# Issuing the load of the next input chunk at the top of a pipelined iteration instead of at its end

## The chip, the cores and the metric

The kernel runs on the eight NeuronCores of one Trainium2 chip. Each core gets two of the sixteen sequences of the input (2 x 2048 rows of 1024 numbers) and works alone; there is no traffic between cores. The metric is the device time in microseconds of the slowest core. A core has a tensor engine (PE), a vector engine (DVE), a scalar engine (ACT), GpSimd (POOL) and a sync engine (SP), which here does nothing but issue DMAs, in the order of its program.

## The reference

```python
xn = _layernorm(x, axis=-1)
s = _L0_attn_ref(xn, Wq, Wk, Wv, Wo)      # 16 heads of 64, causal window of 128, banded softmax
g = _silu(_L0_ffn_ref(xn, rhs))           # rows and columns scaled by absmax/127, rounded, product, rescaled
x = x + s * g
```

In `_L0_attn_ref`, q, k and v are `xn @ W.T`; a chunk of 128 queries looks at its own 128 keys and at the 128 before, under a band mask; the attention output goes through `Wo`. The input is 16 x 2048 x 1024 in float32.

## The kernel before

**Tiling.** A chunk is 128 rows of x, so a core has 32 chunks. All five weight matrices stay in SBUF as bf16. A chunk has five products of 128 x 1024 by 1024 x 1024, each written as 16 matmuls of 128x512: q, k and v (line 461, into `p_proj`, from `wbf`), the quantised product, called ffn (line 461, from `qrhs`), and the output projection, called op (line 565, into `p_av`). Scores (lines 478 and 483, into `p_sc`) and the product of probabilities and values (lines 497 to 506, 64 small matmuls, called AVS) lie between them.

**Order.** There is no scheduler: every engine has its own program, written out by hand, one loop over i from -2 to 33 in each. In iteration i an engine finishes chunk i and prepares chunks i+1, i+2 and i+3. Engines meet at counting semaphores: `W(engine, name, tag)` waits until the counter has reached the value that stands for that step.

- PE: scores of heads 0 to 7 of chunk i, q of i+1, scores of heads 8 to 15, k of i+1, AVS of i, v of i+1, ffn of i+1, op of i. AVS waits for the masks of DVE, v waits for ACT's copy of k out of `p_proj` (line 406), ffn for ACT's copy of v (line 428).
- DVE: the two mask multiplications of chunk i (line 324), reciprocal and scaling of the attention output (lines 329, 333), LN2 of chunk i+2 (lines 256 to 280: inverse deviation by Newton steps on single columns, then the normalised rows `xn`), the ffn product's scaling (342), the combination of chunk i (351, 355: output = x + s g), the gate (362), and LN1 of chunk i+3 (lines 233 to 248: sum, centring, absolute maximum, quantisation factor). LN1 begins with a wait for the load of x of that chunk. LN2 waits for ACT's sum of squares (421).
- ACT: exponentials of the scores (381, 394), copy of q (387), after q's transpose the two copies into zero-padded halves (400, 402), copy of k (406), quantisation of chunk i+2 (415, 418), squares (421), copy of v (428), tanh (433).
- SP: transposes of q (line 174, called trq), of the attention output (180, trao), of k (186, trk), of the quantised rows (194, trql), of the normalised rows (198, trxn), then the store of chunk i (205) and the load of x of chunk i+3 (214). Each waits for the engine that makes its source. All of them lie in one queue.

x has a ring of four slots `XS` in SBUF, chunk c in slot c % 4. The loads of chunks 0, 1 and 2 are issued ahead of the loop.

The helper through which every wait goes is line 126, the one for issues is line 130 to 136.

Of the kernel before, what the change touches and what calls it, by code (L numbers as in the profile page):

```python
# [20 lines left out]
XS = [0, 1024, 2048, 3072]  # L21
# [52 lines left out]
def build(nchunk=NCHUNK):  # L74
    nc = bass.Bass("TRN2", target_bir_lowering=False)
    x_h = nc.dram_tensor("x", [2, 2048, D], F32, kind="ExternalInput").ap()
# [13 lines left out]
    with ExitStack() as es:  # L90
# [3 lines left out]
        scr = sb("scr", [128, SCR_COLS], F32)  # L94
# [26 lines left out]
        def ap3(tensor, cols, off):  # L121
            return bass.AP(tensor, off, [[cols, 128], [128, 8], [1, 128]])

        def W(eng, sname, tag):
            if CUR[0].emit:
                eng.wait_ge(SEMS[sname], CUR[0].tag[(sname, tag)])
# [5 lines left out]
        def I(instr, sname=None, tag=None, n=1):  # L132
            if CUR[0].emit:
                bi = instr()
                if sname is not None:
                    bi.then_inc(SEMS[sname], n)
            if sname is not None:
                CUR[0].inc(sname, n, tag)


        def emit_sync(sync):
            I(lambda: sync.dma_start(mstd[:], mstd_h[:]), "ldw", None, 16)
            I(lambda: sync.dma_start(mc0[:], mc0_h[:]), "ldw", None, 16)
            I(lambda: sync.dma_start(onesc[:], ones_h[:]), "ldw", None, 16)
            I(lambda: sync.dma_start(ident[:], ident_h[:]), "ldw", None, 16)
            I(lambda: sync.dma_start(sel[:], sel_h[:]), "ldw", None, 16)
            I(lambda: sync.dma_start(scr[:, XS[0]:XS[0] + 1024], x_h[0, 0:128, :]),
              "lx0", ("x", 0), 16)
            for i in range(8):
                if i >= 2:  # L150
                    W(sync, "v", ("cast", i - 2))
                wst = WST[i % 2]
                src = rhst_h[i * 128:(i + 1) * 128, :]
                I(lambda src=src, wst=wst: sync.dma_start(scr[:, wst:wst + 1024], src),
                  "ldw", ("ldw", i), 16)
            W(sync, "v", ("cast", 7))
            for ntile in range(8):
                out_ap = bass.AP(qrhs, ntile * 128, [[8192, 128], [1024, 8], [1, 128]])
                in_ap = ap3(bfp2, BFP2_COLS, QRHS_T + ntile * 1024)
                I(lambda o=out_ap, ii=in_ap: sync.dma_start_transpose(o, ii),  # L160
                  "trs", ("trs", ntile), 16)
            for c in (1, 2):
                if c < nchunk:
                    b1, cc1 = divmod(c, 16)
                    I(lambda b1=b1, cc1=cc1, c=c: sync.dma_start(
                        scr[:, XS[c % 4]:XS[c % 4] + 1024],
                        x_h[b1, cc1 * 128:(cc1 + 1) * 128, :]),
                      f"lx{c % 4}", ("x", c), 16)

            for i in range(-2, nchunk + 2):  # L170
                if 0 <= i + 1 < nchunk:
                    c = i + 1
                    W(sync, "a", ("qte", c))
                    I(lambda c=c: sync.dma_start_transpose(
                        ap3(bfp, BFP_COLS, QTF), ap3(bfp, BFP_COLS, QROW)),
                      f"trq{c % 2}", ("trq", c), 16)
                if 0 <= i < nchunk:
                    c = i
                    W(sync, "v", ("ao", c))
                    I(lambda c=c: sync.dma_start_transpose(  # L180
                        ap3(bfp2, BFP2_COLS, AOT[c % 2]), ap3(bfp2, BFP2_COLS, AO[c % 2])),
                      f"trao{c % 2}", ("trao", c), 16)
                if 0 <= i + 1 < nchunk:
                    c = i + 1
                    W(sync, "a", ("kte", c))
                    I(lambda c=c: sync.dma_start_transpose(
                        ap3(bfp, BFP_COLS, KT[c % 2]), ap3(bfp, BFP_COLS, KROW)),
                      f"trk{c % 2}", ("trk", c), 16)
                if 0 <= i + 2 < nchunk:
                    c = i + 2  # L190
                    if i >= 0:
                        W(sync, "t", ("ffn", i))
                    W(sync, "a", ("qbf", c))
                    I(lambda c=c: sync.dma_start_transpose(
                        ap3(bfp, BFP_COLS, QLT[c % 2]), ap3(bfp, BFP_COLS, QB[c % 2])),
                      f"trql{c % 2}", ("trql", c), 16)
                    W(sync, "v", ("xn", c))
                    I(lambda c=c: sync.dma_start_transpose(
                        ap3(bfp, BFP_COLS, XNT[c % 2]), ap3(bfp, BFP_COLS, XN[c % 2])),
                      f"trxn{c % 2}", ("trxn", c), 16)  # L200
                if 0 <= i < nchunk:
                    c = i
                    b, cc = divmod(c, 16)
                    W(sync, "v", ("comb", c))
                    I(lambda b=b, cc=cc, c=c: sync.dma_start(
                        y_h[b, cc * 128:(cc + 1) * 128, :],
                        scr[:, OUTS[c % 2]:OUTS[c % 2] + 1024]),
                      "st", ("store", c), 16)
                if 3 <= i + 3 < nchunk:
                    c = i + 3  # L210
                    if i >= 1:
                        W(sync, "v", ("comb", i - 1))
                    b1, cc1 = divmod(c, 16)
                    I(lambda b1=b1, cc1=cc1, c=c: sync.dma_start(
                        scr[:, XS[c % 4]:XS[c % 4] + 1024],
                        x_h[b1, cc1 * 128:(cc1 + 1) * 128, :]),
                      f"lx{c % 4}", ("x", c), 16)
            if CUR[0].emit:
                sync.wait_ge(SEMS["st"], 16 * nchunk)

# [362 lines left out]
        class FakeEng:  # L583
            def __getattr__(self, name):
                raise RuntimeError("pass-1 must not touch the engine")
        fe = FakeEng()
        emit_sync(fe)
        emit_vector(fe)
        emit_scalar(fe)
# [8 lines left out]
        @block.sync  # L598
        def _(sync):
            emit_sync(sync)  # L600
# [58 lines left out]
```

## Time and profile before

| | us |
|---|---|
| median of 3 runs | 1088.12 (1085.11 to 1091.45) |
| the profiled execution | 1089.02 |
| its span (slowest core, core 6) | 1087.5 |
| spans of the eight cores | 1070.6 to 1087.5 |
| busy on core 6: PE, DVE, ACT | 757.0, 522.6, 424.5 |
| mean granted TensorE clock, cores | 0.906 to 0.912 |

The span runs from the first to the last instruction. Busy shares of engines are averages over the whole span; the clock is a share of 2.4 GHz, so 0.50 is the 1.2 GHz level. A number in square brackets at the end of a timeline row is how long the engine was idle ahead of the instruction, with what ended it. One period of the loop is read from one line of ACT (428, once a chunk) to the same line of the next chunk.

### The profile page before, as it was taken

What the parts mean: (1) busy time and instruction counts of PE and PEld (TensorE: products, weight loads), DVE (VectorE), ACT (ScalarE), POOL (GpSimd) and SP (SyncE); (2) the same over time, 40 slices, a digit from 0 to 9 for tenths busy, and PEclk for the clock granted to TensorE, in tenths of its full rate; (3) what the DMA queues carried; (4) which work ended last, traced back from release to release, by engine and by line L of the source; (5) the groups of instructions that cost most, each with busy time, mean ns of one, the idle gap of its engine ahead of it and who ended that gap; (6) DMA issues with size and microseconds to landing.
All of it is one profiled execution on the core that took longest, in us unless ns stands there. A gap on an engine that the chain in (4) does not pass through costs nothing.

```text
span 1087.5 us, 15213 instructions; the slowest of 8 cores (1070.6 to 1087.5 us)
## 1 busy us (share of the span) xinstructions
PE 757.0 (70%) x5649; PEld 398.9 (37%) x5649; DVE 522.6 (48%) x984; ACT 424.5 (39%) x385; POOL 17.4 (2%) x36
## 2 busy tenths in 40 slices
PE   0001687787787777777788777777877788777794
PEld 0001243343344433434344443444444344433442
DVE  4234254544445544554444554555545544544533
ACT  0001354444334444444443434444444334444441
POOL 6000000000000000000000000000000000000000
PEclk9999998889988988988998988988899988988896
DMA  8964334234433333432434333433233334343321
GB/s 161 186 125 106 79 58 88 71 69 85 87 88 72 75 69 87 88 73 65 88 87 88 82 62 72 88 88 82 67 76 88 87 88 79 74 63 87 88 49 49
DMA packets 193048, 91.40 MB, mean 84 GB/s; under 512 B 179272, under 2 KB 179656, under 8 KB 192976
## 3 DMA queue, kind: packets, MB, share of 16 engines
q1 hardware_dynamic: 188368, 82.04, 34.4%
q0 software_dynamic: 4608, 8.39, 5.2%
q8 instruction: 46, 0.75, 0.3%
q14 instruction: 26, 0.21, 0.1%
HBM read 37.98 MB, written 16.78 MB: 50 GB/s over the span
## 4 chain that ended last, share of the span: by engine, by line
PE 47%; DMA 19%; DVE 19%; ACT 7%; issue 5%; SPq 3%; DVEq 1%; ACTq 0%
PE p_proj L461 28%; DMA scr<-x 11%; PE p_av L565 10%; DMA scr<-rhst 5%; DMA bfp<-bfp 4%; PE p_av L497 4%; PE p_av L503 3%; DVE bfp L324 3%; ACT bfp L428 3%; DVE scr L355 3%; DVE scr L351 3%; DVE sm L243 2%; DVE sm L233 2%; DVE scr L239 2%; SPq L160 1%
## 5 line engine op out<-in xcount | busy, mean ns | idle before, releaser
L461 PE MATMUL p_proj<-wbf,bfp 128*128 128x512 bf16 x1536 | 390.9, 413 | 32.8 <-DMA bfp<-bfp 15.0
L461 PEld LDWEIGHTS p_proj<-wbf,bfp 128*128 128x128 bf16 x1536 | 155.6, 105 | 230.7 <-issue 97.6
L497 PE MATMUL p_av<-bfp 128*128 128x64 bf16 x512 | 81.5, 213 | 146.3 <-DVE bfp L324 143.9
L461 PE MATMUL p_proj<-qrhs,bfp 128*128 128x512 bf16 x512 | 115.6, 379 | 43.8 <-ACT bfp L428 43.8
L497 PEld LDWEIGHTS p_av<-bfp 128*128 128x128 bf16 x512 | 64.4, 126 | 160.3 <-issue 160.0
L565 PE MATMUL p_av<-wbf,bfp 128*128 128x512 bf16 x512 | 118.5, 386 | 5.0 <-DMA bfp<-bfp 5.0
L233 DVE TENSOR_REDUCE sm<-scr 128x1 f32<-128x1024 f32 x32 | 39.0, 1220 | 147.0 <-DMA scr<-x 147.0
L433 ACT ACTIVATE scr<-scr 128x1024 f32<-128x1024 f32 x32 | 33.8, 1056 | 174.1 <-DVE scr L342 174.1
L342 DVE SCALAR_TENSOR_TENSOR scr<-p_proj,sm,scr 128x1024 f32<-128x1024 f32 x32 | 41.1, 1284 | 124.8 <-PE p_proj L461 124.8
L428 ACT CAST bfp<-p_proj 128x1024 bf16<-128x1024 f32 x32 | 32.4, 1012 | 161.6 <-PE p_proj L461 161.6
L461 PEld LDWEIGHTS p_proj<-qrhs,bfp 128*128 128x128 bf16 x512 | 47.8, 97 | 111.6 <-issue 58.6
L381 ACT ACTIVATE bfp<-p_sc 128x2048 bf16<-128x2048 f32 x32 | 60.0, 1877 | 58.5 <-PE p_sc L483 56.3
L503 PE MATMUL p_av<-bfp 128*128 128x64 bf16 x512 | 81.8, 213 | 0.0
L506 PE MATMUL p_sc<-ones_s,bfp 128*128 128x1 bf16 x512 | 81.0, 188 | 0.0
L500 PE MATMUL p_sc<-ones_s,bfp 128*128 128x1 bf16 x512 | 80.8, 188 | 0.0
L415 ACT ACTIVATE q32t<-scr,sm 128x1024 int32<-128x1024 f32 x32 | 36.7, 1148 | 101.9 <-DVE bfp L302 91.9
L351 DVE TENSOR_TENSOR scr<-p_av,scr 128x1024 f32<-128x1024 f32 x32 | 39.2, 1225 | 77.0 <-PE p_av L565 77.0
L565 PEld LDWEIGHTS p_av<-wbf,bfp 128*128 128x128 bf16 x512 | 50.7, 99 | 67.4 <-issue 8.8
L324 DVE TENSOR_TENSOR bfp<-bfp,mstd_s 128x2048 bf16<-128x2048 bf16 x60 | 71.0, 1222 | 4.5 <-ACT bfp L394 4.2
L478 PE MATMUL p_sc<-bfp 128*128 128x128 bf16 x512 | 64.5, 220 | 2.2 <-ACT bfp L381 2.2
L439 PE MATMUL p_av<-ident_s,sm 128*8 128x128 f32 x1 | 0.4, 373 | 94.3 <-DVE bfp L302 94.3
L503 PEld LDWEIGHTS p_av<-bfp 128*128 128x128 bf16 x512 | 65.0, 127 | 0.0
(58 smaller groups left out, 903.6 us busy)
## 6 DMA issues: line engine op xcount, KB each, us to landing
scr<-x SPq DMA_DIRECT2D x32, 512.0 KB, 4.8
y<-scr SPq DMA_DIRECT2D x32, 512.0 KB, 3.0
scr<-rhst SPq DMA_DIRECT2D x8, 512.0 KB
bfp<-bfp SPq DMA_TRANSPOSE x160, 3.3
wbf<-wqt POOLq DMA_DIRECT2D x8, 256.0 KB, 14.9
wbf<-wkt POOLq DMA_DIRECT2D x8, 256.0 KB, 26.1
wbf<-wvt POOLq DMA_DIRECT2D x8, 256.0 KB, 36.5
wbf<-wot POOLq DMA_DIRECT2D x8, 256.0 KB, 47.3
```

Of the source, the lines that this page charges most:

```text
L233: SW(lambda c=c: vector.reduce_sum(sm[:, SUMC:SUMC + 1], scr[:, XS[c % 4]:XS[c % 4] + 1024], AX.X))
L324: I(lambda e=ebv, r=erv, m=mkv: vector.tensor_tensor(e, r, m, ALU.mult), "v", ("e0m" if g == 0 else "e1m", c))
L351: SW(lambda c=c: vector.tensor_tensor(scr[:, T1_:T1_ + 1024], p_av[:, 0:1024], scr[:, GS[c % 2]:GS[c % 2] + 1024], ALU.mult))
L381: I(lambda: scalar.activation(bfp2[:, ERAW:ERAW + 2048], p_sc[:, 0:2048], AF.Exp, scale=0.125), "a", ("e0", c))
L428: I(lambda c=c: scalar.copy(bfp[:, VS[c % 2]:VS[c % 2] + 1024], p_proj[:, 0:1024]), "a", ("vev", c))
L461: mms.append(lambda kc=kc, half=half: tensor.matmul(p_proj[:, half * 512:(half + 1) * 512], lhs_t[:, lhs_base + kc * 128:lhs_base + kc * 1 ...
L478: mms.append(lambda hh=hh, qcol=qcol, tcol=tcol: tensor.matmul(p_sc[:, hh * 256:hh * 256 + 128], bfp[:, ktp + tcol:ktp + tcol + 128], bfp[ ...
L497: mms.append(lambda h=h, e0=e0: tensor.matmul(p_av[:, h * 64:h * 64 + 64], bfp2[:, e0:e0 + 128], bfp[:, vp_ + h * 64:vp_ + h * 64 + 64], s ...
L500: mms.append(lambda h=h, e0=e0: tensor.matmul(p_sc[:, h:h + 1], bfp2[:, e0:e0 + 128], onesc[:], start=True, stop=False))
L503: mms.append(lambda h=h, e0=e0: tensor.matmul(p_av[:, h * 64:h * 64 + 64], bfp2[:, e0 + 128:e0 + 256], bfp[:, vc_ + h * 64:vc_ + h * 64 + ...
L506: mms.append(lambda h=h, e0=e0: tensor.matmul(p_sc[:, h:h + 1], bfp2[:, e0 + 128:e0 + 256], onesc[:], start=False, stop=True))
L565: mms.append(lambda kc=kc, half=half, c=c: tensor.matmul(p_av[:, half * 512:(half + 1) * 512], bfp2[:, AOT[c % 2] + kc * 128:AOT[c % 2] + ...
```

## The change

The block of SP's program that loads x of chunk i+3 moves from the end of iteration i to its start. Its own wait stays the same: slot (i+3) % 4 was last read by the combination of chunk i-1.

```diff
             for i in range(-2, nchunk + 2):
+                if 3 <= i + 3 < nchunk:
+                    c = i + 3
+                    if i >= 1:
+                        W(sync, "v", ("comb", i - 1))
+                    b1, cc1 = divmod(c, 16)
+                    I(lambda b1=b1, cc1=cc1, c=c: sync.dma_start(
+                        scr[:, XS[c % 4]:XS[c % 4] + 1024],
+                        x_h[b1, cc1 * 128:(cc1 + 1) * 128, :]),
+                      f"lx{c % 4}", ("x", c), 16)
                 if 0 <= i + 1 < nchunk:
                     c = i + 1
                     W(sync, "a", ("qte", c))
...
                       "st", ("store", c), 16)
-                if 3 <= i + 3 < nchunk:
-                    c = i + 3
-                    if i >= 1:
-                        W(sync, "v", ("comb", i - 1))
-                    b1, cc1 = divmod(c, 16)
-                    I(lambda b1=b1, cc1=cc1, c=c: sync.dma_start(
-                        scr[:, XS[c % 4]:XS[c % 4] + 1024],
-                        x_h[b1, cc1 * 128:(cc1 + 1) * 128, :]),
-                      f"lx{c % 4}", ("x", c), 16)
```

Only SP's order differs; the programs of PE, DVE, ACT and POOL are the same. In the changed file the load is line 176, and the other lines of SP stand 9 further on: trq 183, trao 189, trk 195, trql 203, trxn 207, the store 214.

SP's queue before, from the transposes of iteration -1 to the first trao and trk of iteration 1:

```order
L174 DMA_TRANSPOSE bfp<-bfp 128x8x128 [waits s_a]
L180 DMA_TRANSPOSE bfp2<-bfp2 128x8x128 [waits s_v]
L186 DMA_TRANSPOSE bfp<-bfp 128x8x128 [waits s_a]
L194 DMA_TRANSPOSE bfp<-bfp 128x8x128 [waits s_t,s_a]
L198 DMA_TRANSPOSE bfp<-bfp 128x8x128 [waits s_v]
L205 DMA y<-scr 128x1024 [waits s_v]
L214 DMA scr<-x 128x1024
L174 DMA_TRANSPOSE bfp<-bfp 128x8x128 [waits s_a]
L180 DMA_TRANSPOSE bfp2<-bfp2 128x8x128 [waits s_v]
L186 DMA_TRANSPOSE bfp<-bfp 128x8x128 [waits s_a]
```

The load in these rows is the one of chunk 3; it stands behind the store of chunk 0. The same stretch of SP's queue after the change (trq, trao, trk, trql and trxn are L183, L189, L195, L203 and L207):

```order
L176 DMA scr<-x 128x1024
L183 DMA_TRANSPOSE bfp<-bfp 128x8x128 [waits s_a]
L189 DMA_TRANSPOSE bfp2<-bfp2 128x8x128 [waits s_v]
L195 DMA_TRANSPOSE bfp<-bfp 128x8x128 [waits s_a]
L203 DMA_TRANSPOSE bfp<-bfp 128x8x128 [waits s_t,s_a]
L207 DMA_TRANSPOSE bfp<-bfp 128x8x128 [waits s_v]
L214 DMA y<-scr 128x1024 [waits s_v]
L176 DMA scr<-x 128x1024 [waits s_v]
L183 DMA_TRANSPOSE bfp<-bfp 128x8x128 [waits s_a]
L189 DMA_TRANSPOSE bfp2<-bfp2 128x8x128 [waits s_v]
L195 DMA_TRANSPOSE bfp<-bfp 128x8x128 [waits s_a]
```

The load of chunk 3 now stands ahead of the first iteration's transposes, and behind the store of chunk 0 stands the load of chunk 4. From there on the kind of every row is the same as before; each load is of one chunk later than the load that stood there. 29 loads (chunks 3 to 31) are moved.

## Rows read from the trace of the kernel before

**Rows 1.** Waits, whole span: engine line <- releaser: us in total, times, longest.
```profile
DVE sm L233 <- DMA scr<-x: 147.0, 31, 8.6
PE p_av L497 <- DVE bfp L324: 143.9, 29, 6.6
ACT bfp L400 <- DMA bfp<-bfp: 68.2, 32, 3.7
```

**Rows 2.** Chain that ended last, one period: start us, us, what.
```profile
634.33 5.02 PE p_proj L461 x16
...
640.70 3.61 PE p_proj L461 x16
644.32 3.47 PE p_av L565 x16
...
651.01 4.81 DMA scr<-x
...
655.92 1.23 DVE sm L233
...
660.12 1.24 DVE bfp L324
661.36 0.24 issue
...
664.30 5.40 PE p_proj L461 x16
```

**Rows 3.** Timeline of ACT, same period: start us, us, instruction, idle before.
```profile
652.21 1.01 ACT L387 CAST bfp<-p_proj 128x1024 bf16<-128x1024 f32 x1 [1.52 <-PE p_proj L461]
...
657.01 1.04 ACT L400 COPY bfp<-bfp 64x1024 bf16<-64x1024 bf16 x1 [1.97 <-DMA bfp<-bfp]
...
659.13 1.01 ACT L406 CAST bfp<-p_proj 128x1024 bf16<-128x1024 f32 x1
```

**Rows 4.** Timeline of ACT, first and last periods: copies of k and v.
```profile
149.47 1.01 ACT L406 CAST bfp<-p_proj 128x1024 bf16<-128x1024 f32 x1
...
154.34 1.01 ACT L428 CAST bfp<-p_proj 128x1024 bf16<-128x1024 f32 x1 [0.29 <-PE p_proj L461]
...
1028.30 1.01 ACT L428 CAST bfp<-p_proj 128x1024 bf16<-128x1024 f32 x1 [5.78 <-PE p_proj L461]
...
1052.27 1.01 ACT L428 CAST bfp<-p_proj 128x1024 bf16<-128x1024 f32 x1 [3.85 <-PE p_proj L461]
```

**Rows 5.** Timeline of PE, iteration 0: v and the start of ffn.
```profile
150.63 3.61 PE L461 MATMUL p_proj<-wbf,bfp 128*128 128x512 bf16 x16 [1.00 <-ACT bfp L406]
155.60 0.59 PE L461 MATMUL p_proj<-qrhs,bfp 128*128 128x512 bf16 x2 [1.36 <-ACT bfp L428]
```

**Rows 6.** Timeline of DVE, iteration -1 to 0: LN1, masks, LN2.
```profile
141.69 1.21 DVE L233 TENSOR_REDUCE sm<-scr 128x1 f32<-128x1024 f32 x1
...
145.89 2.36 DVE L324 TENSOR_TENSOR bfp<-bfp,mc_s 128x2048 bf16<-128x2048 bf16 x2
...
154.15 0.15 DVE L256 TENSOR_SCALAR sm<-sm 128x1 f32<-128x1 f32 x1 [2.82 <-ACT scr L421]
```

**Rows 7.** Timeline of DVE, the period of rows 2: the gate.
```profile
650.42 1.22 DVE L362 SCALAR_TENSOR_TENSOR scr<-scr 128x1024 f32<-128x1024 f32 x1
```

**Rows 8.** Timeline of SP's queue, iteration 0: trxn.
```profile
158.67 1.23 SPq L198 DMA_TRANSPOSE bfp<-bfp  x1
```

**Rows 9.** Stretches: length, PE busy (instructions), granted clock, DMA share, GB/s.
```profile
148.00:149.00 1.00, 1.00 (x42) 1.00 0.00 0
611.00:623.00 12.00, 12.00 (x79) 1.00 0.37 90
657.00:661.00 4.00, 0.00 (x0) 1.00 0.00 0
662.00:663.00 1.00, 1.00 (x30) 0.50 0.09 16
```

**Rows 10.** Line 461 over the whole span: ns min/median/max, first and last start.
```profile
L461 PE MATMUL p_proj<-wbf,bfp x1536: 376/379/634, 113.9 to 1051.8; 128*128 128x512 bf16 x192
```

## The prediction

> **What bounds the kernel now.** I read the totals of waits first. The vector engine (DVE) waits 147.0 us for loads of x at line 233, and the tensor engine (PE) waits 143.9 us at AVS for the masks of DVE [rows 1]. The two totals are nearly alike, about 4.7 and 5.0 us a time, which suggests one cause seen from two engines. The chain of waits shows it for one period [rows 2]: op ends at 647.79 (644.32 + 3.47), the load of x is issued at 651.01 and takes 4.81, LN1 begins at 655.92, the first mask at 660.12, and AVS at 661.60 (after 0.24 of issue). In program order DVE has LN1 of chunk i+3 ahead of the masks of chunk i+1, so a load issued too late for LN1 holds masks that need nothing of it. DVE had been free since 651.64 [rows 7].
>
> The length of a period comes from ACT's copy of v: from 154.34 to 1028.30 there are 29 periods [rows 4], so 873.96 / 29 = 30.14 us each. The last period, 1028.30 to 1052.27, has no load and no LN1 and takes 23.97 [rows 4].
>
> A second loss hangs on the first. PE is idle from 657 to 661 at a granted clock of 1.00 (2.4 GHz), and in 662 to 663, inside AVS, the clock is 0.50 (1.2 GHz) [rows 9]. It comes back only within the v product: from v to ffn this period needs 640.70 - 634.33 = 6.37 us [rows 2], while in iteration 0, where the clock stayed at 1.00 in AVS [rows 9], it was 155.60 - 150.63 = 4.97 [rows 5]. That is 1.40 us.
>
> **The change, part by part.** It removes and adds no instruction. It moves 29 DMA issues, and of the other engines none. Queued behind the moved load is the whole of SP's program. Its wait, for the combination of chunk i-1, is one that the store just ahead of it has already waited for, so in the loop it adds no waiting. Between the store and the next trq there stands one load before and one after; only its chunk is one later. So the loop's DMA traffic keeps its places, and I price the move itself at 0 per period. Bounds: if it added one more issue on trq's way it would cost the 0.4 us or less that lies between neighbouring issues; it could give that back too. The one load really added at a new place is that of chunk 3, ahead of iteration 0's trq; it could hold that trq by a load's time at most, 4.81 us once [rows 2], and not by less than 0. I take 0, because PE and SP are still in iteration -1 when it goes, and keep 5 us for the range.
>
> What goes is LN1's wait, since the load is issued a period earlier. Now the new period, counted from the end of op (0). DVE frees itself at 651.64 - 647.79 = 3.85 [rows 2, 7]. LN1 takes 660.12 - 655.92 = 4.20 and the first mask 1.24 [rows 2], to 9.29; with 0.24 of issue AVS could start at 9.53. What is late next? The k product: the copy of q ends at 653.22, which is 5.43 after op [rows 3]; with a start 0.15 later (the same step as from line 406 to v, 150.48 to 150.63 [rows 4, 5]) and 3.61 of work, it ends at 9.19. So AVS starts at 9.53, and even at its length of now, 2.70 (661.60 to 664.30), it ends at 12.23.
>
> Then v waits for ACT's copy of k, and this path sets the end:
> - op's end to the end of the copy of q: 5.43.
> - From there to the start of line 400, which is trq's trip: 653.22 to 657.01 is 3.79 with 1.97 of idle [rows 3]. Over all chunks the idle time is 68.2 / 32 = 2.13 [rows 1], so 3.79 + 0.16 = 3.95.
> - Lines 400, 402 and 406, 657.01 to 660.14: 3.13 [rows 3]. To v: 0.15.
> - So v starts at 12.66, 0.43 after AVS. v to ffn at full clock: 4.97 [rows 5]. ffn and op, 640.70 to 647.79: 7.09 [rows 2].
>
> Sum: 5.43 + 3.95 + 3.13 + 0.15 + 4.97 + 7.09 = 24.72 us, against 30.14. The saving is 5.42, of which 1.40 is the clock and 4.02 the masks. Of the 147.0 us of wait about 4.0 of each 4.7 turn into time; the rest is the new wait for the copy of k.
>
> Three things were hidden by LN1's wait and stand nearly bare now. They happened in iteration 0, where x was there already (LN1 starts at 141.69 without a wait [rows 6]), so their room can be read there, counted from the end of the copy of k, 150.48:
> - The copy of v waits 0.29 for PE [rows 4], so ACT is just in time.
> - LN2 now waits for the squares of ACT (2.82, beginning at 154.15 [rows 6]). The normalised rows leave for trxn at 158.67 [rows 8], which is 8.19. ffn ends at 0.15 + 4.97 + 3.61 = 8.73, so DVE is ready for it.
> - trxn is issued at 8.19; with the trip of trq, 3.79, it has landed by 11.98. The next q starts at 0.15 + 4.97 + 7.09 + (652.21 - 647.79 - 3.61 = 0.81) = 13.02. It has 1.0 us left, where today it has over 4.
>
> The clock: in the new period PE is idle for 0.34 ahead of AVS, at most 1.3 ahead of v, and 1.36 between v and ffn, nowhere the 4 us after which it fell. A 12 us stretch in which PE was busy throughout has a clock of 1.00 [rows 9]. The Trainium skill, "TensorE: Matmul & The Clock Gate" (Part 1: The HAM clock gate), has a rule that speaks against this: with three or more cores of a die in dense matmuls, a peak-current limiter takes the die to 13/16 of the clock. The trace doesn't show it, though all eight cores run dense stretches; by the rule, as an estimate from that page, four products on the path would each be 16/13 as long, about 3.2 us more a period and some 1025 us in all.
>
> **The sum.** 29 periods x 5.42 = 157.1 us. The periods at both ends and the tail behind the last one stay. The profiled execution took 1089.0, so 1089.0 - 157.1 = 931.9: I forecast 932 us. The median of the runs shown is 1088.1, less than 0.1% away, and is not corrected for.
>
> A check: the last period, 23.97, is nearly the new one with trq alone on the queue. All periods like that would give 1089.0 - 29 x 6.17 = 910, which is the lower bound.
>
> **Rivals.**
> 1. The clock still falls once a period, because AVS is light work for PE or the remaining gaps count. Then v to ffn stays at 6.37, the period is 26.12 and the time 1089.0 - 29 x 4.02 = 972. For it: the clock is at 0.50 in just this place now. Against it: it was 1.00 in AVS of iteration 0.
> 2. The transfers collide more. trq shares SP's queue with the load just ahead of it, and the loop asks for the same bytes in less time. If every trq idled like the longest, 3.7 instead of 2.13 [rows 1], that is 1.57 a period: 932 + 46 = 978.
> 3. Power, in part: PE on all cores is busier, and the clock drops within the products. A matmul of line 461 lasts 634 ns at worst against 379 [rows 10]; 16 of them are 4.1 us a product, and four products on the path 16.3 us a period. With a sixth of that work at 1.2 GHz the period grows by 2.7, to 1011 us. The skill's limiter would be this rival.
> 4. The other side, slower: the same mechanism, in more than a third of the products' work (5.42 / 16.3); at all of it the time is 932 + 29 x 16.3 = 1405. For it speaks only that the chip has never shown a loop with so little idle time here; against it the 12 us at 1.00 [rows 9].
> 5. The change does nothing, because the masks are really released by ACT: line 406 ends at 660.14 [rows 3], the first mask starts at 660.12 [rows 2]. Then the time is 1089. Against it: a mask waits only for an exponential, and in iteration 0 the masks (145.89 [rows 6]) came well ahead of line 406 (149.47 [rows 4]).
>
> **Chances.** Forecast 0.72 (its own range 915 to 952: the bound below with the 5 us, and 0.7 us a period above), clock 0.10, collisions 0.06, power in part 0.06, slower 0.02, nothing 0.03, something else that is still faster 0.01. A measurement of this kernel tells a change of about 0.5% from none. Faster by more: 0.72 + 0.10 + 0.06 + 0.06 + 0.01 = 0.95; within: 0.03; slower: 0.02. The range of 915 to 978 holds the first three cases for the most part, and leaves out power, nothing and slower.
>
> **What would show it.** Right: the wait of line 233 for x is near zero in the loop; PE's long wait at AVS for masks falls below 1 us a time; PE now waits for ACT's copy of k (line 406) ahead of v, some 0.4 to 1.3 us a time; DVE waits for the squares at line 256; the clock is 1.00 throughout the loop; the copy of v comes every 24.7 us. Wrong: a clock under 1.00 in the loop (rivals 1, 3, 4), a wait at line 400 well over 2.1 us (rival 2), or a q product that waits for trxn, which the margin of 1.0 us should prevent.

## The result: 946.1 us where 932 was forecast, and the profile after

| | before | after |
|---|---|---|
| median of 10 runs each, us | 1087.4 (1082.7 to 1091.5) | 946.1 (942.3 to 948.8) |
| ratio, 95% interval | | 0.870 (0.868 to 0.872) |
| the profiled execution, us | 1089.0 | 946.2 |
| its span, slowest core | 1087.5 (core 6) | 944.7 (core 5) |
| spans of the cores | 1070.6 to 1087.5 | 933.1 to 944.7 |
| mean granted clock | 0.906 to 0.912 | 0.969 to 0.973 |

The kernel is 13.0% faster. The time lies in the stated range (915 to 978), 14 us above the point. In the sessions of the experiments some executions took longer with one die at a lower granted clock (one of e3 1025.0 us against 925.1), and every median below leaves them out. The waits of the changed kernel on core 5, whole span, are the first thing to read (who waited, for whom, us in total, times, longest):

```profile
DVE sm L256 <- ACT scr L421: 101.4, 31, 16.8
...
ACT bfp L400 <- DMA bfp<-bfp: 63.9, 32, 3.4
...
PE p_proj L461 <- ACT bfp L406: 33.8, 32, 2.7
...
DVE sm L233 <- DMA scr<-x: 13.0, 2, 7.6
...
PE p_av L497 <- DVE bfp L324: 8.7, 29, 0.6
```

Against [rows 1], the wait of line 233 for x went from 147.0 to 13.0 us and happens only twice, ahead of the loop; the wait of AVS for the masks went from 143.9 to 8.7, at most 0.6 a time. In their place stand the two waits that the prediction named: PE for the copy of k (line 406) and DVE for the squares of ACT (line 256).

The chain that ended last shows one period, from the copy of v to the copy of v (start, us, what):

```profile
233.00 1.02 ACT bfp L428
...
234.26 3.61 PE p_proj L461 x16
237.88 3.45 PE p_av L565 x16
...
242.22 3.47 PE p_proj L461 x16
...
245.77 1.02 ACT bfp L387
...
246.85 3.56 DMA bfp<-bfp
...
251.54 1.04 ACT bfp L402
...
252.61 1.02 ACT bfp L406
...
253.77 3.63 PE p_proj L461 x16
...
257.47 1.02 ACT bfp L428
```

The load of x, LN1 and the masks, which stood in the chain of [rows 2], aren't in it. The path is the one of the sum: ffn, op, q, copy of q, trq, lines 400 to 406, v. This period is 24.47 us. Not all are. Two neighbouring v products of the timeline of PE, and the granted clock in stretches that hold them (columns as in rows 9):

```profile
227.60 5.30 PE L461 MATMUL p_proj<-wbf,bfp 128*128 128x512 bf16 x16 [1.05 <-ACT bfp L406]
...
253.77 3.61 PE L461 MATMUL p_proj<-wbf,bfp 128*128 128x512 bf16 x16 [0.94 <-ACT bfp L406]
```

```profile
155.00:886.00 731.00, 643.06 (x5106) 0.97 0.43 94
...
227.00:228.00 1.00, 0.40 (x2) 1.00 0.00 0
228.00:231.00 3.00, 3.00 (x9) 0.51 0.51 98
...
250.00:258.00 8.00, 6.17 (x83) 1.00 0.29 56
```

The clock still fell to 1.2 GHz, now in 11 of the 29 periods on cores 4 and 5 and in 9 on the other six, and not during AVS but at the start of v. Ahead of this v PE had been idle for 1.05 us only; over all 11 falls of core 5 that gap was 1.04 to 2.40 us, and in its 18 other periods 0.29 to 0.99. On the other cores falls came with gaps from 0.39 us on. On core 5 such a v takes 5.1 to 5.3 us instead of 3.6. Both ends of the loop on core 5 are in the timeline of ACT, from which the mean period is (886.22 - 155.40) / 29 = 25.20 us:

```profile
155.40 1.01 ACT L428 CAST bfp<-p_proj 128x1024 bf16<-128x1024 f32 x1 [0.29 <-PE p_proj L461]
...
886.22 1.01 ACT L428 CAST bfp<-p_proj 128x1024 bf16<-128x1024 f32 x1 [0.29 <-PE p_proj L461]
```

### The profile page after: what moved, and what is told of

It is laid out like the page before. It is cut to its first block, busy times and chain, and to the rows that moved or that the text cites. A ratio compares the mean times of both kernels' runs of the same rounds, so it can differ in the third digit from the quotient of the medians.

```text
span 944.7 us, 15213 instructions; the slowest of 8 cores (933.1 to 944.7 us)
## 1 busy us (share of the span) xinstructions
PE 719.6 (76%) x5649; PEld 373.9 (40%) x5649; DVE 522.7 (55%) x984; ACT 424.5 (45%) x385; POOL 17.4 (2%) x36
## 4 chain that ended last, share of the span: by engine, by line
PE 52%; DMA 18%; ACT 15%; issue 6%; DVE 5%; SPq 2%; ACTq 0%; DVEq 0%
PE p_proj L461 37%; DMA bfp<-bfp 13%; PE p_av L565 12%; DMA scr<-rhst 6%; ACT bfp L402 4%; ACT bfp L406 3%; ACT bfp L428 3%; ACT bfp L387 3%; PE p_sc L478 1%; PE p_sc L483 1%; SPq L160 1%; DVE sm L292 1%; ACT bfp L400 1%; DVE scr L297 1%; DVE q32t L300 1%
## 5 line engine op out<-in xcount | busy, mean ns | idle before, releaser
L461 PE MATMUL p_proj<-wbf,bfp 128*128 128x512 bf16 x1536 | 369.4, 396 | 62.7 <-ACT bfp L406 33.8
L461 PEld LDWEIGHTS p_proj<-wbf,bfp 128*128 128x128 bf16 x1536 | 149.6, 101 | 246.4 <-issue 100.9
L381 ACT ACTIVATE bfp<-p_sc 128x2048 bf16<-128x2048 f32 x32 | 60.0, 1876 | 58.5 <-PE p_sc L483 56.3
L497 PE MATMUL p_av<-bfp 128*128 128x64 bf16 x512 | 61.4, 190 | 11.7 <-DVE bfp L324 8.7
L478 PE MATMUL p_sc<-bfp 128*128 128x128 bf16 x512 | 64.0, 219 | 2.2 <-ACT bfp L381 2.2
L483 PE MATMUL p_sc<-bfp 128*128 128x128 bf16 x512 | 64.0, 219 | 0.0
L400 ACT COPY bfp<-bfp 64x1024 bf16<-64x1024 bf16 x32 | 33.5, 1046 | 63.9 <-DMA bfp<-bfp 63.9
L503 PE MATMUL p_av<-bfp 128*128 128x64 bf16 x512 | 61.4, 190 | 0.0
L256 DVE TENSOR_SCALAR sm<-sm 128x1 f32<-128x1 f32 x32 | 4.9, 154 | 101.4 <-ACT scr L421 101.4
L394 ACT ACTIVATE bfp<-p_sc 128x2048 bf16<-128x2048 f32 x32 | 60.1, 1877 | 1.4 <-PE p_sc L483 1.4
L497 PEld LDWEIGHTS p_av<-bfp 128*128 128x128 bf16 x512 | 49.5, 97 | 27.4 <-issue 24.7
```

The costliest lines, as they stand in the source:

```text
L381: I(lambda: scalar.activation(bfp2[:, ERAW:ERAW + 2048], p_sc[:, 0:2048], AF.Exp, scale=0.125), "a", ("e0", c))
L394: I(lambda: scalar.activation(bfp2[:, ERAW + 2048:ERAW + 4096], p_sc[:, 0:2048], AF.Exp, scale=0.125), "a", ("e1", c))
L400: I(lambda c=c: scalar.copy(bfp[0:64, QTM[c % 2]:QTM[c % 2] + 1024], bfp[0:64, QTF:QTF + 1024]))
L461: mms.append(lambda kc=kc, half=half: tensor.matmul(p_proj[:, half * 512:(half + 1) * 512], lhs_t[:, lhs_base + kc * 128:lhs_base + kc * 1 ...
L478: mms.append(lambda hh=hh, qcol=qcol, tcol=tcol: tensor.matmul(p_sc[:, hh * 256:hh * 256 + 128], bfp[:, ktp + tcol:ktp + tcol + 128], bfp[ ...
L483: mms.append(lambda hh=hh, qcol=qcol, tcol=tcol: tensor.matmul(p_sc[:, hh * 256 + 128:hh * 256 + 256], bfp[:, ktc + tcol:ktc + tcol + 128] ...
```

## The experiments

Two questions were open: is it the order on DVE that made the late load dear, and where are the 14 us? All kernels were timed beside the kernel before on the same chip (medians of before: 1086.8 us for the first four, 1086.5 for the last four).

### e1: masks ahead of LN1, the load left where it was

```diff
                         "v", ("e0m" if g == 0 else "e1m", c))
+                if 0 <= i + 2 < nchunk and i >= 0:
+                    LN1(i + 2)
...
-                if 0 <= i + 3 < nchunk and i >= -1:
-                    LN1(i + 3)
```

> The load of x stays where it was in the kernel before; instead DVE does the masks of a chunk ahead of LN1. My theory: the late load cost time only because LN1 stood in front of the masks on DVE. Then the masks no longer wait, the second one starts when the exponential is there (7.3 us after op), LN1 runs from about 8.6 to 12.8 after op, and PE waits for the copy of k as in the changed kernel: a period of 24.8 to 25.3 us and 942 to 955 us in all, though the wait of line 233 for x doesn't go to zero. Rival (it is the arrival of x itself that bounds the loop, wherever LN1 stands): the time stays over 1050 us.

Measured: 960.5 us, ratio 0.883 (0.881 to 0.886). Its waits, on the slowest core as in every experiment:

```profile
DVE bfp L324 <- ACT bfp L394: 75.1, 32, 2.5
...
PE p_proj L461 <- ACT bfp L406: 53.9, 32, 3.0
...
ACT q32t L415 <- DVE sm L248: 17.9, 29, 1.1
DVE sm L233 <- DMA scr<-x: 14.9, 8, 6.4
```

With the load as late as before, 126 of the 141 us are won. So the cost of the late load was the queue on DVE: masks stood behind an LN1 that nobody needed yet. The second mask's wait for its exponential (75.1) covers the arrival of x, which is why even line 233 hardly waits; I had expected it to. The mean period of the slowest core is 25.72 against 25.20, which is the 14 us to the changed kernel. Less than half of that is the clock, which fell 10 to 16 times a core here, against 9 to 11. The rest is in periods without a fall: their mean over all cores is 24.8 us here and 24.4 in the changed kernel, some 10 us in 29 periods. Part of it is that ACT's quantisation (line 415) now waits for LN1's factor (line 248), 0.6 us a time, and so comes later to its copy of v. The median is some 5 us above the range that I gave.

### e2: the kernel before, with PE kept busy while it waits

```diff
+            def FILL(n):
+                for _ in range(n):
+                    I(lambda: tensor.matmul(p_sc[:, 512:1024], wbf[:, 0:128],
+                                            wbf[:, 0:512], start=True, stop=True))
...
                     W(tensor, "a", ("e1", c))
+                    FILL(16)
                     W(tensor, "v", ("e0m", c))
```

> The kernel before, with 16 matmuls of 128x512 whose result nobody reads, issued on PE ahead of its wait for the masks; they take some 3.5 us of its 4.5 us of idle time. It separates the clock's part from the part of the masks. My theory: the clock stays at 2.4 GHz, v to ffn goes from 6.3 to about 5.0 us and AVS from 2.7 to about 2.0, both on the path here, so 2.1 us x 29 = 61 us less: about 1027 us. Rival A (AVS is light work and lets the clock fall by itself now and then, as in the changed kernel): a third of the falls stay, 1040 to 1050 us. Rival B (the clock's fall costs nothing, all was the masks): 1088 us.

Measured: 1034.3 us, ratio 0.952 (0.948 to 0.955). The stretch of the loop, the waits, and the filling matmuls on the timeline of PE:

```profile
155.00:960.00 805.00, 726.50 (x5549) 0.99 0.41 86
```

```profile
DVE sm L233 <- DMA scr<-x: 128.6, 31, 5.7
...
PE p_av L502 <- DVE bfp L324: 29.5, 29, 2.6
```

```profile
420.96 3.62 PE L492 MATMUL p_sc<-wbf 128*128 128x512 bf16 x16
```

DVE waits for x nearly as long as before, and PE still can't begin AVS; but 512 matmuls that compute nothing make the kernel 52 us faster, and the clock in the loop is 0.99 where it was 0.90 (in the kernel before, 154 to 1028 us). The periods came down as expected (27.93 us on the slowest core, 2.2 less). Of these 2.2 us the mean AVS gives 0.6 (2.1 instead of 2.7) and v to ffn 1.1 (5.25 instead of 6.36), which is the clock. The other 0.5 is as much as the loads land sooner: 4.3 us after their issue instead of 4.8. The last iteration, where the 16 matmuls hide behind nothing, costs some 6 us, which I had left out, and 2 to 6 falls of 29 a core stay. So of the 141 us about 50 (1.7 x 29) are to be had by the clock alone.

### e3: the changed kernel, PE kept busy between AVS and v

```diff
                     AVS(c, 1)
+                    FILL(3)
```

> The changed kernel, with 3 matmuls of 128x512 whose result nobody reads between AVS and v, in the gap in which PE waits for the copy of k (0.3 to 1.0 us). In the changed kernel the clock still falls in a third of the periods, about 3 us after AVS has begun. Theory 1 (the idle gaps beside AVS count): the falls go, 0.6 us x 29 = 17 us less, 929 us. Theory 2 (AVS itself is light enough): the falls stay and the time stays at 943 to 948 us.

Measured: 925.1 us, ratio 0.851 (0.848 to 0.853), so 21 us below the changed kernel, where 17 were expected. The loop's stretch on the slowest core, and its waits for trq:

```profile
156.00:860.00 704.00, 640.65 (x5189) 1.00 0.43 97
```

```profile
ACT bfp L400 <- DMA bfp<-bfp: 54.8, 32, 3.2
```

No core has more than one fall left in the loop. Theory 2 is out: AVS alone doesn't let the clock fall. Theory 1 fits, but filling takes idle time away and adds dense work at once, and e3 can't tell the two apart. e4 below speaks for the idle time: with no filling and a shorter gap it has few falls too. There is a gain I didn't expect: line 400 waits 54.8 us in all instead of 63.9, that is 0.3 us a period.

### e4: the load behind trq

```diff
-                if 3 <= i + 3 < nchunk:            # the load's block
...
                     I(lambda c=c: sync.dma_start_transpose(
                         ap3(bfp, BFP_COLS, QTF), ap3(bfp, BFP_COLS, QROW)),
                       f"trq{c % 2}", ("trq", c), 16)
+                if 3 <= i + 3 < nchunk:            # the load's block
```

> The changed kernel, with the load of x issued behind trq in place of ahead of it. Theory: trq shares the queue and the DMA engines with the load ahead of it, and its trip (3.8 us on the slowest core) is on the path through the copy of k; with the load behind it the trip falls to 3.2 to 3.3, 0.55 us x 29 = 16 us less, and with a shorter gap ahead of v the clock falls less often: 922 to 932 us. Rival (the trip is trq's own or comes from other cores' traffic): 943 to 948 us. If the load now delays the transposes behind it: over 950 us.

Measured: 917.6 us, ratio 0.844 (0.842 to 0.847): the fastest kernel of this study. Its waits for trq, a period on ACT's timeline, and the load's row among the DMA issues (KB each, median us to landing):

```profile
ACT bfp L400 <- DMA bfp<-bfp: 50.6, 32, 3.2
```

```profile
418.38 1.01 ACT L428 CAST bfp<-p_proj 128x1024 bf16<-128x1024 f32 x1 [0.28 <-PE p_proj L461]
...
431.16 1.01 ACT L387 CAST bfp<-p_proj 128x1024 bf16<-128x1024 f32 x1 [1.52 <-PE p_proj L461]
...
435.41 1.05 ACT L400 COPY bfp<-bfp 64x1024 bf16<-64x1024 bf16 x1 [1.42 <-DMA bfp<-bfp]
...
442.39 1.01 ACT L428 CAST bfp<-p_proj 128x1024 bf16<-128x1024 f32 x1 [0.29 <-PE p_proj L461]
```

```profile
scr<-x SPq DMA_DIRECT2D x32, 512.0 KB, 4.2
```

trq's trip is 435.41 - 432.17 = 3.24 us here, 3.3 on average (3.8 with the load ahead of it), and the period 24.01. The theory holds, but the time is 4 us below the range that I gave. The gap ahead of v is shorter (0.43 us in periods without a fall, on the slowest core), and only 0 to 3 falls a core are left; I had expected fewer falls, but not so few. The load itself lands in 4.2 us instead of 4.8. That isn't shown to be trq's doing: in e3, where load and trq are issued as in the changed kernel, the load lands in 4.3.

What trq waits for can be read from the landings. In the changed kernel on core 5, chunks 3 to 29, it lands 0.85 to 1.30 us after the load ahead of it, whether that load took 4.3 us or 6.3. So it ends behind the load, and its trip is as long as the load makes it.

### e5: store and load behind trq; e8: the same, with one filling matmul

```diff
+                if 0 <= i - 1 < nchunk:
+                    c = i - 1
...                                                # store of chunk i-1, then the load, behind trq
-                if 0 <= i < nchunk:
-                    c = i
...                                                # store of chunk i at the end of the iteration
                     AVS(c, 1)
+                    FILL(1)                        # e8 alone
```

> The changed kernel, with the store of y and the load of x both issued behind trq. Theory: trq then has the queue to itself, as in the last period of the kernel before, whose length was 23.97 us; with the load alone behind trq the periods were 24.06 to 24.34, so 0.1 to 0.3 us x 29 = 3 to 9 us less than that kernel: 909 to 915 us. Rival (the store never touched trq; or the store, now later, holds the combination of the chunk after the next): 916 to 921 us or more.

> As the kernel with store and load behind trq, and one matmul of 128x512 that nobody reads between AVS and v. If falls of the clock are left there, they go, at 0.6 us or less a period: 905 to 914 us. If none is left, the same time as without it within 3 us.

Measured: e5 919.5 us, ratio 0.846 (0.844 to 0.848); e8 921.8, ratio 0.848 (0.845 to 0.850). Both are the same as e4 within the noise; e8 missed its 905 to 914. ACT of e5:

```profile
434.72 1.01 ACT L387 CAST bfp<-p_proj 128x1024 bf16<-128x1024 f32 x1 [1.52 <-PE p_proj L461]
...
438.96 1.04 ACT L400 COPY bfp<-bfp 64x1024 bf16<-64x1024 bf16 x1 [1.41 <-DMA bfp<-bfp]
```

The trip is 438.96 - 435.73 = 3.23 us, as in e4, and an ordinary period 24.0. The rival was right: the store doesn't touch trq. In e4 it is issued 2.72 us ahead of trq and takes 2.66, so it has landed when trq is issued. What raises the mean period of these kernels to 24.1 to 24.3 are one to three periods of 26 to 28 us a core, most with a longer trip and a fall of the clock; the extra matmul doesn't remove them. The longer trips have a companion. In the trip of 4.28 us on e5's slowest core a packet of the instruction queue moved beside trq (DMA queues, 627.77 to 631.9: packets, MB, share of the engines):

```profile
q8 instruction: 1, 0.02, 1.4%
```

Over all cores of e4, e5 and e8 (chunks 2 to 30) 51 trips took over 3.9 us, and in 45 of them a 16 KB packet of an instruction queue moved; of the other 645 trips 5 had one. No run changed the code's loading, so that it is the cause isn't shown.

### e6: the copy of k ahead of the wait for trq

```diff
+                    W(scalar, "t", ("k", c))
+                    if c >= 1:
+                        Wv(scalar, f"trk{(c - 1) % 2}", 16 * ((c - 1) // 2 + 1))
+                    I(lambda: scalar.copy(bfp[:, KROW:KROW + 1024], p_proj[:, 0:1024]),
+                      "a", ("kte", c))
                     Wv(scalar, f"trq{c % 2}", 16 * (c // 2 + 1))
```

> The changed kernel, with ACT's copy of k moved ahead of its wait for trq and of the two copies behind it. In the changed kernel PE waits for this copy ahead of v. If that wait is the only bound, v starts when AVS ends, 1.0 us earlier: 1.0 x 29 = 30 us and the falls of the clock beside it, 17 us, so 900 to 916 us. My theory: ACT's own program is a bound of the same length (from trq's landing through lines 400, 402, 406, 415, 418, 421 to the copy of v, 16.1 us after op, against 16.3 for the end of v), so only 0.2 us x 29 = 6 us come back from the move, and 5 to 10 us more since a v at half clock now has room: 928 to 936 us.

Measured: 926.3 us, ratio 0.854 (0.851 to 0.857). ACT on its slowest core (here line 402 is the copy of k, 405 and 407 are the two behind trq, 430 is the copy of v):

```profile
420.22 1.01 ACT L402 CAST bfp<-p_proj 128x1024 bf16<-128x1024 f32 x1 [2.09 <-PE p_proj L463]
421.13 1.04 ACT L405 COPY bfp<-bfp 64x1024 bf16<-64x1024 bf16 x1
422.18 1.04 ACT L407 COPY bfp<-bfp 64x1024 bf16<-64x1024 bf16 x1
423.25 1.15 ACT L417 ACTIVATE q32t<-scr,sm 128x1024 int32<-128x1024 f32 x1
424.49 1.06 ACT L420 ACTIVATE bfp<-q32t 128x1024 bf16<-128x1024 int32 x1
425.64 1.06 ACT L423 ACTIVATE scr<-scr 128x1024 f32<-128x1024 f32 x1
426.60 0.19 ACT L423 ACTIVATION_READ_ACCUMULATOR scr<-scr 128x1 f32 x1
426.69 0.99 ACT L430 CAST bfp<-p_proj 128x1024 bf16<-128x1024 f32 x1
```

From the copy of k to the copy of v ACT has no idle time at all, where the changed kernel's copy of v waited 0.29 for PE. That is my theory, not the rival by which 30 us would come back: ordinary periods fell from 24.4 to 24.1, and the rest of the 20 us is the clock. It falls 4 to 6 times a core, and at another place: v follows AVS at once, and PE's long gap now lies between v and ffn, so that the ffn product is the slow one (5.3 us instead of 3.6). The timeline of PE shows it once:

```profile
549.11 5.30 PE L463 MATMUL p_proj<-qrhs,bfp 128*128 128x512 bf16 x16 [2.54 <-ACT bfp L430]
```

A period with a fall is 1.7 us longer than one without; on core 5 of the changed kernel it is 2.2, because trq's trip is 0.6 longer in those periods too. I had expected 928 at the least.

### e7: the load moved for odd chunks alone

```diff
+                if 3 <= i + 3 < nchunk and i % 2 == 0:      # the block at the top
...
-                if 3 <= i + 3 < nchunk:
+                if 3 <= i + 3 < nchunk and i % 2 == 1:      # the block at the end
```

> The kernel before, with the load moved to the top of the iteration for odd chunks alone. Then every second period has two loads ahead of trq (the store, the late load of an even chunk, the early one of the next odd chunk), and the other one has none. Theory (a trq waits for the loads ahead of it on the queue): the periods with none take 24.0 to 24.5 us; in the others LN1 waits as before and trq's trip grows from 3.8 to about 8 us, so that v starts 16.5 to 17 us after op, with a fallen clock: 29 to 31 us. Mean 27, so 1089 - 29 x 3.1 = about 998 us, with 985 to 1015 allowed. Rival (loads don't hold trq; each moved load saves its own 4.9 us): (1088 + 946) / 2 = 1017 us with trips of 3.8 in all periods.

Measured: 1006.5 us, ratio 0.926 (0.924 to 0.929). Two periods of ACT (lines stand 9 further on: 396 is the copy of q, 409 waits for trq, 437 is the copy of v):

```profile
484.57 1.01 ACT L437 CAST bfp<-p_proj 128x1024 bf16<-128x1024 f32 x1 [4.79 <-PE p_proj L470]
...
497.35 1.01 ACT L396 CAST bfp<-p_proj 128x1024 bf16<-128x1024 f32 x1 [1.52 <-PE p_proj L470]
...
501.58 1.05 ACT L409 COPY bfp<-bfp 64x1024 bf16<-64x1024 bf16 x1 [1.41 <-DMA bfp<-bfp]
...
508.57 1.01 ACT L437 CAST bfp<-p_proj 128x1024 bf16<-128x1024 f32 x1 [0.29 <-PE p_proj L470]
...
521.34 1.01 ACT L396 CAST bfp<-p_proj 128x1024 bf16<-128x1024 f32 x1 [1.52 <-PE p_proj L470]
...
527.84 1.04 ACT L409 COPY bfp<-bfp 64x1024 bf16<-64x1024 bf16 x1 [3.66 <-DMA bfp<-bfp]
...
539.25 1.01 ACT L437 CAST bfp<-p_proj 128x1024 bf16<-128x1024 f32 x1 [4.72 <-PE p_proj L470]
```

The periods alternate: 24.00 us with no load in the way (trip 3.22) and 30.68 with two loads ahead of trq and LN1 waiting (trip 5.49). The trip grows with the loads ahead of it: 3.2, 3.7, 5.5 us for none, one and two. It doesn't reach 8 us. The two loads and trq of the second period among the DMA issues (519 to 522.3 and 522.4 to 524 us; KB each, median us to landing):

```profile
scr<-x SPq DMA_DIRECT2D x2, 512.0 KB, 5.7
```

```profile
bfp<-bfp SPq DMA_TRANSPOSE x1, 5.3
```

The loads are issued at 520.15 and 520.63, and trq at 522.43. The second load lands 6.20 us after its issue, at 526.83, and trq at 527.76, 0.93 later. Over all such periods of this core the median is 0.94. So trq does end behind both loads, but most of the 3.1 us from issue to landing that it takes alone passes while they still move. My 8 us had added the two.

## Why the prediction was right, and where the 14 us are

**What goes.** Right. LN1's wait and the idle time ahead of AVS went as stated. e1 confirms the reason, the order on DVE, by removing it without the move, and with the same gain but for some 14 us.

**What is late next.** Right. The sum let v start 12.66 us after op, and not AVS but ACT's copy of k release it. In the period shown, op ends at 241.33 (237.88 + 3.45) and v starts at 253.77, which is 12.44. The three bare margins also came as read from iteration 0: the copy of v waits for PE for 0.29 us, and DVE waits for the squares for some 2.8 a period. PE never waited for trxn in the loop.

**Moving the issue costs nothing in the loop.** Right on balance, and it held a hidden cost that the sum carried in its term of 3.95 for trq's trip: that is 3.3 when the load isn't ahead of it (e4). The term was measured right (3.81 now), but I took it as given, when moving the load past trq as well was worth another 28 us together with the clock. The one load at a new place, chunk 3's, cost nothing, as forecast: on core 5 it is issued at 136.77 and has landed at 141.10, and the trq behind it is issued at 145.27 and takes 3.22. (The two listings of SP's queue above show iteration 0 and the start of iteration 1, not the transposes of iteration -1.)

**The clock.** Here the term was wrong. "v to ffn at full clock: 4.97" was to hold in every period, since PE was nowhere idle for the 4 us after which the clock had fallen, and at most for 1.3 us ahead of v. On core 5 the mean is 5.59: 18 periods at 4.97 and 11 at 6.46 to 6.66. Rival 1 happened in a third of the periods. The gap ahead of v went up to 2.4 us there, but 6 of the 11 falls came with one of 1.04 to 1.15. My evidence against it was one AVS at full clock in iteration 0; it showed that a fall isn't certain, not that it doesn't happen. The Trainium skill, "TensorE: Matmul & The Clock Gate" (Part 1: The HAM clock gate), says of the window in which the clock's monitor looks that "it doesn't reset when your kernel starts". The trace is in keeping with it: on core 0 periods with a gap of 0.39 to 1.17 us ahead of v have a fall, and others with one of 0.48 to 1.06 have none.

**The ledger of core 5.** Predicted period 24.72; clock +0.62; trip 3.81 instead of 3.95, -0.14; together 25.20, as measured. 29 x (25.20 - 24.72) = 13.9 us of the 14.3 between 931.9 and 946.2. The remaining 0.4 is the sum of a start 1.1 later and an end 0.7 shorter.

**Power (rivals 3 and 4).** Nothing of it in the profiled executions: with PE busy for 0.91 of a stretch (640.65 of 704) in e3 the granted clock was 1.00. The 13/16 of the Trainium skill's page (the same section) doesn't show there. The price of 4.1 us a product in these rivals was too high, since it took the longer duration of a matmul for the distance of two starts. In the slow v at 381.45 us on core 5 starts lie 0.43 us apart instead of 0.21, so that a product wholly at 1.2 GHz would take some 3.5 us more (16 x 0.22), an estimate from these two.

**Split of the gain.** About 50 us of the 141 can be had by the clock alone (e2). By e1, 126 come from taking the masks out from behind LN1, which brings most of that clock with it. The parts overlap and don't add up.

**Open.** Why loads land 0.5 us sooner in the kernels in which the clock seldom falls (4.3 us in e2 and e3 against 4.8), though the same bytes move at the same places, wasn't settled; trq, which lands about 1 us behind the load, is quicker with it. Nor was it settled whether a fall needs idle time or only little dense work.

## What to carry to other kernels

A late transfer costs what stands behind its waiting instruction in the same engine's order: look for work there that doesn't need it, and either move that work ahead or issue the transfer a period earlier; one of them does. After such a change look at what stands behind the transfer in its queue: here taking the load out from ahead of a transpose on the path brought another 28 us, a fifth of the first gain. When an idle stretch of PE goes, don't book the full clock for every period as long as light work and gaps of 1 us remain (here a third of the periods had a fall); a few matmuls for nothing in the gap tell in one run what the clock still costs.

## What the runs showed of the hardware that I had not expected

- The clock fell to 1.2 GHz in about a third of the periods, though for 65 of the 76 falls in the changed kernel no idle gap of PE over 1.4 us stood around AVS (64 small matmuls, 2.04 us). AVS came before each fall, with a gap of at most 0.6 us ahead of it and one of 0.4 to 2.6 us behind. 0.65 us of filling between AVS and v left none or one a core (e3).
- A DMA transpose issued 2.3 us behind a 512 KB load landed about 1 us after the load, however long that took: its trip was 3.8 us on average on the slowest core, and 3.2 with the load behind it (e4). With two loads ahead it was 5.5 us (e7).
- The store, issued 2.7 us ahead of the transpose and landed before the transpose was issued, did not slow it at all (e4 against e5: 3.24 and 3.23 us).
- Where nothing else stood in trq's way (e4, e5, e8), 45 of the 51 trips over 3.9 us had a 16 KB instruction packet moving beside them.
